# Sliding-window attention, re-ordered into rounds of two units: both units' value products together, all full-array products together

## The reference

```python
q = (x @ Wq.T + bq).reshape(B, S, H, HD).transpose(0, 2, 1, 3)
k = (x @ Wk.T + bk).reshape(B, S, HK, HD).transpose(0, 2, 1, 3)   # v likewise; k, v repeated 8 times
scores = jnp.einsum('bhqd,bhkd->bhqk', q, k) * scale
allowed = (qi >= kj) & (qi - kj < WINDOW)
scores = jnp.where(allowed[None, None], scores, neg)
logits = jnp.concatenate([scores, sink], axis=-1)
probs = jax.nn.softmax(logits, axis=-1)[..., :-1]
o = jnp.einsum('bhqk,bhkd->bhqd', probs, v)
return o.transpose(0, 2, 1, 3).reshape(B, S, H * HD) @ Wo.T + bo
```

## Time and profile before

| what | value |
|---|---|
| median of 3 runs | 4065.85 us (4062.46 to 4073.61) |
| profiled execution, its own time | 4065.05 us |
| span of the profiled execution | 4063.3 us |
| TensorE busy in the span | 3736.1 us (92%) |
| VectorE, ScalarE, GpSimd busy | 3194.1, 2258.0, 1293.7 us |
| mean granted TensorE clock | 0.949 |
| scores of the attention (line 479), first to last start | 43.9 to 1559.5 us |

### The profile page before, as it was taken

How to read it: one execution, slowest core, us unless ns; L and a number is a source line. 1 busy time by engine, 2 the same in 40 slices (tenths; PEclk the granted TensorE clock), 3 DMA queues, 4 the chain that set the end, 5 groups by cost and what they waited for, 6 DMA issues and landing times.

```text
span 4063.3 us, 77870 instructions
## 1 busy us (share of the span) xinstructions
PE 3736.1 (92%) x24958; PEld 2497.5 (61%) x24958; DVE 3194.1 (79%) x11911; ACT 2258.0 (56%) x6991; POOL 1293.7 (32%) x1099
## 2 busy tenths in 40 slices
PE   7999999999999999999998996998986999899955
PEld 5777777777777776666664433334555666555543
DVE  7888888888888886667777995776886778788771
ACT  5878777777777775225765443433333222367611
POOL 2333333333333332003544884550000000222116
PEclk9999999999999998997998998998996999899968
DMA  2000000000000000321000000000000000000023
GB/s 123 2 2 2 2 2 2 2 2 2 2 2 2 2 2 29 92 77 64 2 2 1 1 0 11 1 1 1 1 1 33 1 1 1 1 33 2 14 63 50
DMA packets 30835, 63.56 MB, mean 16 GB/s; under 512 B 3424, under 2 KB 19808, under 8 KB 29152
## 3 DMA queue, kind: packets, MB, share of 16 engines
q1 hardware_dynamic: 24288, 52.29, 3.7%
q0 software_dynamic: 6144, 6.30, 0.9%
HBM read 49.93 MB, written 8.65 MB: 14 GB/s over the span
## 4 chain that ended last, share of the span: by engine, by line
PE 70%; DVE 16%; issue 6%; ACT 5%; POOL 2%; DMA 1%; DVEq 0%; POOLq 0%; ACTq 0%; SPq 0%
PE ps L479 9%; PE ps L518 9%; PE ps L176 8%; PE ps L460 6%; PE ps L503 5%; PE ps L1596 3%; PE ps L1567 3%; PE ps L1565 3%; PE ps L2220 2%; PE ps L2207 2%; DVE gbbc L2259 2%; PE ps L936 2%; DVE gbbc L2248 2%; DVE gbbc L2254 2%; PE ps L914 2%
## 5 line engine op out<-in xcount | busy, mean ns | idle before, releaser
L604 DVE CUSTOM_DVE_ANT_0 T<-ps,C 128x128 f32<-128x128 f32 x2048 | 451.2, 285 | 1.9
L751 POOL TENSOR_TENSOR W<-W,T 128x512 f32<-128x512 f32 x256 | 260.7, 1039 | 525.5 <-DVE T L640 525.5
L698 ACT ACTIVATE W<-T 128x128 f32<-128x128 f32 x1024 | 396.0, 391 | 46.2 <-DVE T L625 46.2
L751 POOL TENSOR_TENSOR T<-T 128x512 f32<-128x512 f32 x256 | 260.8, 1039 | 484.8 <-DVE T L640 484.8
L479 PE MATMUL ps<-T 64*128 64x128 f32 (+1 forms) x4096 | 405.5, 338 | 4.0 <-DVE T L604 3.0
L479 PEld LDWEIGHTS ps<-T 64*128 64x128 f32 x4096 | 344.7, 187 | 85.4 <-issue 64.5
L698 ACT ACTIVATE T<-T 128x128 f32<-128x128 f32 x1024 | 396.2, 391 | 0.3 <-DVE T L625 0.2
L518 PE MATMUL ps<-W,gbbc 128*64 128x256 f32 x3072 | 388.1, 388 | 3.2 <-ACT T L715 3.2
L615 DVE COPY_PREDICATED W<-gbbc,ps 128x512 f32<-128x512 int32 x512 | 342.6, 721 | 38.7 <-PE ps L176 38.7
L176 PE MATMUL ps<-C,T 128*128 128x128 f32 (+1 forms) x1620 | 261.1, 298 | 49.7 <-DVE T L307 19.0
L1163 POOL TENSOR_TENSOR QK<-T,QK 128x512 fp32r<-128x512 f32 x128 | 161.9, 1274 | 379.6 <-ACT T L1123 261.3
(11 more groups left out here) (417 smaller groups left out, 8701.1 us busy)
## 6 DMA issues: line engine op xcount, KB each, us to landing
T<-crow_dram SPq DMA_DIRECT2D x128, 128.0 KB, 3.0
W<-in_l1f_dram SPq DMA_DIRECT2D x1, 6152.0 KB, 18.9
W<-in_l0a_dram SPq DMA_DIRECT2D x1, 5172.5 KB, 25.4
W<-in_l2f_dram SPq DMA_DIRECT2D x1, 3160.0 KB, 10.1
W<-in_l3f_dram SPq DMA_DIRECT2D x1, 3076.0 KB, 9.7
W<-in_sm_dram SPq DMA_DIRECT2D x1, 2729.0 KB, 9.6
W<-in_l0f_dram SPq DMA_DIRECT2D x1, 2256.0 KB, 30.1
X<-in_x_dram SPq DMA_DIRECT2D x1, 2048.0 KB, 7.9
```

Source lines behind the costliest of these rows:

```text
L604: done(e.tensor_tensor_reduce(sm[:, at:at + 128], src, m, 1.0, -3.0e38, ALU.add, ALU.max, mx[:, col:col + 1]), s["masked"], x == (3 if ban ...
L698: done(e.activation(a.Pr[i % 4][:, at:at + w_], a.Sm[i % 2][:, at:at + w_], ACT.Exp, bias=a.ngs[i % 4][:, c:c + 1], scale=a.scale, accum_o ...
L751: e.tensor_tensor(pr, pr, a.rins[i % 4][:, c:c + 4].unsqueeze(2).broadcast_to([P, 4, 128]), ALU.mult).then_inc(s["norm"].sem, 1)
```

## The change

A round is now a group, not a unit. In round n TensorE does the scores of unit 2n, the values of both units of group n-2, the scores of unit 2n+1, and then all products that use the whole array: transposes of unit 2(n-1), q0 of group n+1, `out` of group n-2, in even rounds kv of group n+2, transposes of unit 2(n-1)+1, q1 of group n+1. The two value results go to banks 3 and 5 in turn (before: bank 5), and the transposes of even units to banks 4 and 3, of odd ones to 5 and 4 (before: 3 and 4). The queues of VectorE and ScalarE are re-ordered to match. The copies of the keys are made by GpSimd. The diff, cut to its core; the checks that a group exists, which stand ahead of each step, and the removed old rounds are left out:

```diff
@@ plan
-    a.Sb, a.Tb, a.Ob, a.side, a.acc = b_[0:3], b_[3:5], b_[5], b_[6], b_[7]
+    a.Sb, a.side, a.acc = b_[0:3], b_[6], b_[7]
+    a.Ob = b_[3], b_[5]
+    a.Tb = (b_[4], b_[3]), (b_[5], b_[4])
...
-TURN_LAG = 3
-VALUES_LAG = 4
+def attention_ahead(a, n):
+    out = [("q0", n + 1)] if n + 1 < a.groups else []
+    out += [("kv", n + 2)] if n % 2 == 0 and n + 2 < a.groups else []
+    return out + ([("q1", n + 1)] if n + 1 < a.groups else [])
 def attention_rounds(a):
+    for n in range(a.groups + 2):
+        group = lambda lag: n - lag if 0 <= n - lag < a.groups else None
+        ahead = n + 1 if n + 1 < a.groups else None
+        kv = n + 2 if n % 2 == 0 and n + 2 < a.groups else None
+        yield group(0), group(1), group(2), ahead, kv
@@ TensorE: transposes of a unit
+    def turn(i):
+        for c in range(2):
+            e.wait_ge(*s["norm"](2 * i + c + 1))
+            if c == 0 and i % 2 == 0:
+                past(e, s["even"], i)
+            elif c == 0 or i % 2 == 0:
+                past(e, s["o"], i - 1)
+            else:
+                e.wait_ge(*s["odd"](2 * i))
@@ TensorE: values of a unit
-        past(e, s["o"], i)
+        e.wait_ge(*s["odd"](2 * i + 2))
+        e.wait_ge(*s["even"](i + 1))
         for c in range(3):
-            e.wait_ge(*(s["odd"](2 * i + c + 1) if c < 2 else s["even"](i + 1)))
@@ TensorE: a round (each step only if its group exists)
+        scores(2 * n)
+        values(2 * leaving)
+        values(2 * leaving + 1)
+        scores(2 * n + 1)
+        turn(2 * turning)
+        project("q0", ahead)
+        out(leaving)
+        project("kv", kv)
+        turn(2 * turning + 1)
+        project("q1", ahead)
...
@@ VectorE: keys and values of a pair of groups
-            c_.hold(e)
-            c_.then(e.tensor_copy(kt[0:64, 256:512], kt[64:128, 0:256]))
-            e.tensor_copy(kt[64:128, 256:512], kt[0:64, 0:256]).then_inc(s["keys"].sem, 1)
@@ VectorE: a round (likewise)
+            project("q1", n)
+            masks(2 * n)
+            shift(2 * n)
+            inverse(2 * turning + 1)
+            masks(2 * n + 1)
+            parted(2 * turning)
+            shift(2 * n + 1)
+            project("kv", kv)
...
+            e.wait_ge(*s["out"](leaving + 1))
+            past(e, s["yread"], b)
+            e.tensor_scalar(a.yT, a.acc[:, 0:256], w["bo"], ga, ALU.add, ALU.mult).then_inc(s["y"].sem, 1)
+            parted(2 * turning + 1)
+            inverse(2 * n)
...
+            e.wait_ge(*s["yread"](b + 1))
+            e.tensor_tensor(x, x, a.acc[:, 0:256], ALU.add).then_inc(s["x"].sem, 1)
...
@@ ScalarE: a round (likewise)
+            weights(2 * turning + 1, 2, 8)
+            sinks(2 * turning + 1)
+            outputs(2 * leaving)
+            begin(2 * n)
+            weights(2 * n, 0, 3)
+            outputs(2 * leaving + 1)
+            weights(2 * n, 3, 6)
+            turned(2 * turning)
+            project(ahead)
+            weights(2 * n, 6, 8)
+            sinks(2 * n)
+            begin(2 * n + 1)
+            weights(2 * n + 1, 0, 2)
+            turned(2 * turning + 1)
@@ GpSimd
+    def both(n):
+        kt = a.kT[n // 2 % 2]
+        e.wait_ge(*s["free"](a.uses["kv", n] + 1))
+        past(e, s["norm"], 4 * n - 6)
+        c_.then(e.tensor_copy(kt[0:64, 256:512], kt[64:128, 0:256]))
+        c_.hold(e)
+        e.tensor_copy(kt[64:128, 256:512], kt[0:64, 0:256]).then_inc(s["keys"].sem, 1)
+        e.wait_ge(*s["keys"](n // 2 + 1))
+    both(0)
     for i in range(a.units):
...
+        if i % 4 == 0 and i // 2 + 2 < a.groups:
+            both(i // 2 + 2)
```

More of the change, by code:

```diff
@@ L481, in scores, with out @@
             done(m, s["early"], (p, qt, j) == (0, 0, 1))
[L483 to L497, removed]
+    def turn(i):
[7 more added lines that the diff above has]
+                e.wait_ge(*s["odd"](2 * i))
+            for h in range(4):
+                at = 512 * c + 128 * h
+                done(transpose(k, e, a.Tb[i % 2][c][:, 128 * h:128 * h + 128], a.Pr[i % 4][:, at:at + 128]), s["turn"],
+                     h == 3)
+    def out(n):
         b, g = divmod(n, a.nG)
[L499 to L502, removed]
+        past(e, s["x"], b)
+        e.wait_ge(*s["o"](2 * n + 2))
+        for c in range(a.CH):
             done(e.matmul(a.acc[:, 0:256], w["wo"][:, (g * a.CH + c) * 128:(g * a.CH + c + 1) * 128],
@@ L522, in attention_pe @@
         project(step, 0)
[L523 to L546, removed]
+    for n, turning, leaving, ahead, kv in attention_rounds(a):
+        if n is not None:
+            scores(2 * n)
+        if leaving is not None:
+            values(2 * leaving)
+            values(2 * leaving + 1)
+        if n is not None:
+            scores(2 * n + 1)
+        if turning is not None:
+            turn(2 * turning)
+        if ahead is not None:
+            project("q0", ahead)
+        if leaving is not None:
+            out(leaving)
+        if kv is not None:
+            project("kv", kv)
+        if turning is not None:
+            turn(2 * turning + 1)
+        if ahead is not None:
+            project("q1", ahead)
+        if leaving is not None and leaving % a.nG == a.nG - 1:
+            e.wait_ge(*s["y"](leaving // a.nG + 1))
+            for j in range(2):
+                done(transpose(k, e, a.acc[:, 128 * j:128 * j + 128], a.yT[:, 128 * j:128 * j + 128]), s["yread"], j == 1)
 def attention_dve(k, a, e):
@@ L567, in project @@
         e.wait_ge(*s["side"](a.uses[step, n] + 1))
-        past(e, s["half"], 6 * (n - 1))
+        past(e, s["half"], 6 * (n - 1) if step == "q1" else 6 * (n - 2))
         if step == "q1":
@@ L640, in inverse @@
         e.reciprocal(rin, den).then_inc(s["inv"].sem, 1)
[L642 to L678, removed]
@@ new lines, in masks @@
+    def masks(i):
+        past(e, s["exps"], i - 1)
+        past(e, s["shift"], i - 3)
+        merge(i, 1)
+        merge(i, 0)
+        mask(i, 1)
+        mask(i, 0)
+        mask(i, 2)
+    project("kv", 0)
+    for n, turning, leaving, ahead, kv in attention_rounds(a):
+        if n is not None:
+            project("q1", n)
+            masks(2 * n)
+            shift(2 * n)
+        if turning is not None:
+            inverse(2 * turning + 1)
+        if n is not None:
+            masks(2 * n + 1)
+        if turning is not None:
+            parted(2 * turning)
+        if n is not None:
+            shift(2 * n + 1)
+        if kv is not None:
+            project("kv", kv)
+        last = leaving is not None and leaving % a.nG == a.nG - 1
+        b = leaving // a.nG if last else 0
+        if last:
+            ga = k.modT[:, 96 * a.l + 32 + b:96 * a.l + 33 + b]
+            e.wait_ge(*s["out"](leaving + 1))
+            past(e, s["yread"], b)
+            e.tensor_scalar(a.yT, a.acc[:, 0:256], w["bo"], ga, ALU.add, ALU.mult).then_inc(s["y"].sem, 1)
+        if turning is not None:
+            parted(2 * turning + 1)
+        if n is not None:
+            inverse(2 * n)
+        if last:
+            x = k.X[:, 256 * b:256 * b + 256]
+            e.wait_ge(*s["yread"](b + 1))
+            e.tensor_tensor(x, x, a.acc[:, 0:256], ALU.add).then_inc(s["x"].sem, 1)
+            e.wait_ge(*s["x"](b + 1))
+            stats(k, e, 2 * b)
+            stats(k, e, 2 * b + 1)
```

70 lines of the change are left out of this document (26 added, 44 removed).

## The result

The changed kernel takes 4047.07 us (median of 11 runs, 4041.57 to 4066.91) against 4075.59 us (median of 11, 4062.38 to 4091.82): ratio 0.9944, interval 0.9928 to 0.9959. Both are true, and the reader has to look inside to see why: the attention is 14.5 us shorter in the trace, and a later layer gave it back in this one execution.

The account below looks back on a forecast made before the run. TensorE's own sequence was taken to bound the attention, so only shortening it could gain. Shape changes -44, wait behind kv +23, masks at sequence ends +9, ends +1: -11 from 4065.85, giving 4055 us, range 4038 to 4080.

Parts of the forecast that it names:

- The gain: TensorE's full rounds: four changes of array shape instead of six, 0.35 us less a group, -44 us over 126 groups.
- D: Rival: TensorE's step from values to scores costs 0.1 us more, total 4067.5 us; chance 0.10.
- E: Rival: changes of array shape bring a third of the gain, 15 us, with all costs, total 4084 us; chance 0.03.
- The wait behind kv: q1 waits for VectorE to read kv from the shared bank: 0.365 us in 62 rounds, +23 us.
- B: Rival: no wait shows at q1 behind kv, kv read out sooner or weights early, total 4032 us; chance 0.10.
- The pause at a sequence's end: Second scores wait 0.60 us for masks because VectorE adds to X late; fifteen sequences, +9 us.
- Masks: Second scores wait for the first's masks: slack 0.25 us, no pause taken, bounds 0 to 0.25 a group.
- C: Rival: masks late in every round, VectorE's merge over 0.25 us late; at 0.5 late 4086 us; chance 0.17.
- The copies' worth: Key copies moved from VectorE to GpSimd gain nothing, as VectorE was not the bound; 0.7 us a copy on GpSimd.
- The ends: First rounds +5 us for waits, last rounds -4 us; net +1, bounds -4 and +7.
- The pauses leave the clock alone: Waits at the attention's start and end do not lower TensorE's clock: both end windows have 1.00.
- within 0.3%: Whole kernel's time within 0.3% of before, between 4053.6 and 4078.1 us; chance 0.50, against 0.35 faster and 0.15 slower.

Follow-up runs that it names:

- q0_between: Changed kernel with q0 of each round moved between the two sets of values, adding two changes of array shape; ratio to the kernel before 1.0121.
- kv_next_q1: Changed kernel with kv moved behind the odd unit's transposes, so nothing lies between kv and q1; ratio to the kernel before 1.0095.
- split_out: Changed kernel with the last of the four products of `out` moved behind kv; ratio to the kernel before 0.9930.
- add_later: Changed kernel with VectorE's sequence-end addition to X and statistics moved behind the next round's first masks and shift; ratio to the kernel before 0.9952.
- copies_back: Changed kernel with the two key copies given back to VectorE, behind its reads of kv; ratio to the kernel before 0.9987.
- changed again: The changed kernel measured once more with no edit; ratio to the kernel before 0.9946.

## Why the prediction was right, step by step

The gain and both waits came where the prediction put them, which the middle of the attention shows: it had -44, +23 and +9 there, measured are -44, +19 and +8. The time as such was less well foreseen. The prediction's -11 us of 4065.85 is a ratio of 0.9973, outside the measured interval of 0.9928 to 0.9959, and the medians differ by 28.5 us. That 4047 us lies in its range is owed to the width of the range too, and that the attention's -14.5 came within 4 us of the -11 is in part luck: the ends were off in both directions, as told below.

**The gain was right.** Plain rounds of 11.11 as written, 0.35 less a group, 44 us over 126. In the middle it is 124 rounds: -43.4, with +18.3 behind kv, +7.7 at the sequences' ends and -0.9 for one kv fewer in this stretch, which is the -18.3 read there. q0_between shows the same 0.35 from the other side. D, a dearer step from values to scores, and E, the changes of shape at a third of that price, fall with it.

**The wait behind kv was in the right place and 20% too large.** The round with kv is 12.29, not 12.35: 12.29 - 11.11 - 0.88 = 0.30 instead of 0.365, 19 us over 62, not 23. The release and read of kv were right, as VectorE's rows show, after a kv that starts at 268.10:

```profile
269.18 0.48 DVE L579 TENSOR_SCALAR T<-ps,T 128x256 f32<-128x256 f32 x1 [0.86 <-PE ps L460]
269.58 0.41 DVE L582 TENSOR_TENSOR gbbc<-ps,W 128x256 f32<-128x256 f32 x1
```

The bank is free at 269.99, K + 1.89 (predicted K + 1.90). The step that was off is the 0.15 from there to the first matmul, taken from the attention's last product: here q1 starts 0.06 later, at 270.05. It is not the length of the wait that makes the two differ, for in kv_next_q1, where TensorE had been idle for 0.91, q1 again starts 252.70 - (252.23 + 0.41) = 0.06 after the end of the read:

```profile
252.23 0.41 DVE L582 TENSOR_TENSOR gbbc<-ps,W 128x256 f32<-128x256 f32 x1
```

The last section has what does. q1 takes 0.10 more for its late weights where I had 0.075. kv_next_q1 and split_out show that the pause is this read. B falls.

**The pause at a sequence's end** was there, 12.78 - 12.29 = 0.49 where I had 0.60. The merge came when I said: the last two transposes end at 258.40, the scores start at 258.33 and the merge at 260.49, or 2.16 into them (predicted 2.13):

```profile
258.02 0.38 PE L176 MATMUL ps<-C,gbbc 128*128 128x128 f32 x2
258.33 1.58 PE L484 MATMUL ps<-T 64*128 64x128 f32 x16
```

From the merge to the second scores it was 263.07 - 260.49 = 2.58 where I had 2.72, and that is the difference. Over fifteen sequences this is 8 us, not 9. add_later shows that VectorE's work on X was the cause.

**Masks.** No pause in any other round, so C fell. The slack was 0.39, not 0.25: copies_back starts the merge 0.57 later and pays 0.18. The term of 2.47 + 0.1 from merge to seen masks was the part mis-sized: 277.64 - 275.07 = 2.57 with TensorE's start in it, where I had 2.72.

**The copies' worth was wrong.** "The key copies leave VectorE, which was not the bound, and get nothing" holds in the old order (1.0002). In the new one, left on VectorE, they cost 11 us: nearly four fifths of the attention's 14.5 us hang on that part of the change. The step that failed is that I costed the move from the trace of the old order, though the paragraph on kv had found VectorE's chain behind kv at its limit. The same numbers give it: K + 4.47 and 0.58 more is 0.68 after what the scores allow, over the slack of 0.25 or, as measured, of 0.39. GpSimd's copies took 0.39 us each (I had taken 0.7); nothing waits for them.

**The ends** cost +3 by difference (-14.5 + 44.1 - 18.6 - 7.7), inside the bounds of -4 and +7, where I had +1. The start, read as a length, cost 8.9 where I had 5, and the end gave 5.1 where I had 4. "The pauses leave the clock alone: both end windows have 1.00" failed: the windows were those of the old order's ends, and in the new order's first rounds the clock's mean was 0.75. That was worth some 2.5 of the 8.9 us.

**The sum.** -11 predicted, -14.5 in the trace of the attention, -18 at equal clock, -23 by the ratio. The first difference is the two over-sized pauses less the ends. The 3.5 us between -14.5 and -18 are, by the estimate above, clock of the first rounds that the line counts as chance. The last would be clock of later layers, which no step of the prediction had as a term; as the first set has no clocks for the kernel before, that stays argued. The forecast put the most on "within 0.3%"; the ratio is outside it, on the side given 0.35.

## What to carry to other kernels

Where an engine is never idle, read its sequence for what the same step costs in two places: here a step behind another of the same array shape was 0.05 to 0.16 us shorter, and grouping by shape was worth 0.35 us a group before a single wait was touched. Then list what each moved step had stood behind: each shared bank needs as much other work between its two uses as its reader takes, and that can be dealt out, as the fourth product of `out` behind kv did. A part that "gets nothing" by the old trace is to be costed once more in the new order, in the chain that the change has made tight.

## What was unexpected of the hardware

- In the attention TensorE starts 0.05 or 0.15 us after the end of the instruction that it waited for, and never in between. From 80 to 1600 us the ten traces have 98 waits with 0.052 to 0.056, after idle times of 0.17 to 2.70 us, and 219 with 0.144 to 0.148, after 0.10 to 0.79 us; VectorE and ScalarE end waits of both kinds. What tells them apart in every one of these cases is where the trace has the wait: on the step's first weight load itself (0.05), or on a semaphore instruction of its own ahead of that load (0.15), which a step has when it waits for more than one semaphore.
- The time of later layers moves with the granted clock by 2.9 us for 0.001 of its mean, and its means go from 0.939 to 0.952 over these runs. Positions within the attention, where the clock was full, told changes below 1 us, where the intervals of the ratios are 6 to 9 us to either side.
- In four of the traces (changed, changed again, split_out, kv_next_q1), once, at the end of the eighth sequence, the second scores waited for 0.79 instead of 0.42; in the changed kernel VectorE stood there for 0.27 us ahead of q1, which the waits put down to the scores on TensorE. copies_back and q0_between have such a round of 0.3 to 0.4 us too much elsewhere, the two kernels with the later addition to X have none. Why it is only there is open.
